# A four-layer gated decoder: tile weights of the first mixture of experts loaded inside the attention before it, and the router's steps rearranged

## What is computed

```python
def _L0_xattn_ref(Q_decoder, K_encoder, V_encoder, Wq, bq, ...):   # 16 heads of 8
    ...
    attn = jax.nn.softmax(scores, axis=-1)
    ...
def _L0_ffn_ref(x, router_w, w1, w2):        # 8 experts, 128 -> 512 -> 128
    probs = jax.nn.softmax(xf @ router_w.T, axis=-1)
    topv, topi = jax.lax.top_k(probs, 2)
    topv = topv / (topv.sum(axis=-1, keepdims=True) + 1e-09)
    cw = (jax.nn.one_hot(topi, e, dtype=xf.dtype) * topv[..., None]).sum(axis=1)
    h = jax.nn.gelu(jnp.einsum('td,edh->teh', xf, w1), approximate=False)
    y = jnp.einsum('teh,ehd->ted', h, w2)
    out = jnp.einsum('te,ted->td', cw, y)
x = x + jnp.tanh(g_xattn[0]) * _L0_xattn_ref(_layernorm(x, axis=-1), ctx_1024, ctx_1024, ...)
x = x + jnp.tanh(g_ffn[0]) * _L0_ffn_ref(_layernorm(x, axis=-1), ...)
```

## Time and profile before

| | us |
|---|---|
| median of 3 runs | 1693.77 (1693.45 to 1694.56) |
| the profiled execution | 1691.46 |
| its span from first to last instruction | 1689.7 |
| busy: PE / DVE / POOL / ACT | 1406.0 / 1081.6 / 780.9 / 681.7 |
| mean granted clock of TensorE | 0.925 of full |

### The profile page before, as it was taken

How to read it: one execution, slowest core, us unless ns; L and a number is a source line. 1 busy time by engine, 2 the same in 40 slices (tenths; PEclk the granted TensorE clock), 3 DMA queues, 4 the chain that set the end, 5 groups by cost and what they waited for, 6 DMA issues and landing times. The chain is left out here.

```text
span 1689.7 us, 34140 instructions
## 1 busy us (share of the span) xinstructions
PE 1406.0 (83%) x10919; PEld 1116.2 (66%) x10919; DVE 1081.6 (64%) x2418; ACT 681.7 (40%) x1663; POOL 780.9 (46%) x1037
## 2 busy tenths in 40 slices
PE   4999765989656785999978886899999999687996
PEld 3777655989655564666634444777878778587884
DVE  4888752414399687999958884455555855364455
ACT  3676442323343333556633332344455454421121
POOL 2554581345384353555533331444444577307355
PEclk9999897999855897999979999899999999889899
DMA  6400015758110000000000000000000000186952
GB/s 183 179 2 2 11 34 158 220 170 265 54 33 10 1 1 1 0 0 0 0 1 0 0 0 1 1 0 0 0 1 1 6 20 15 54 235 188 275 163 83
DMA packets 96487, 100.03 MB, mean 59 GB/s; under 512 B 12150, under 2 KB 69678, under 8 KB 95727
## 3 DMA queue, kind: packets, MB, share of 16 engines
q1 hardware_dynamic: 62322, 69.60, 13.6%
q0 software_dynamic: 8192, 16.79, 3.4%
q10 hardware_dynamic: 25852, 12.09, 2.5%
HBM read 72.23 MB, written 26.21 MB: 58 GB/s over the span
## 5 line engine op out<-in xcount | busy, mean ns | idle before, releaser
L439 POOL TENSOR_TENSOR exp_scores<-exp_scores,softmax_recip 128x308 f32<-128x308 f32 x256 | 181.7, 742 | 179.8 <-DVE softmax_recip L611 179.6
L633 PE MATMUL psum<-identity,exp_scores 128*77 128x128 f32 x1024 | 164.7, 287 | 37.6 <-POOL exp_scores L439 25.4
L1942 POOL TENSOR_TENSOR exp_scores_xattn<-exp_scores_xattn,softmax_recip_xattn 128x1640 f32<-128x1640 f32 x32 | 93.5, 2921 | 162.6 <-DVE softmax_recip_xattn L2115 162.6
L1201 PE MATMUL psum<-sorted_transposed_ffn,tile_weights_up_ffn 128*128 128x128 f32 x1280 | 164.7, 283 | 4.3 <-DVE sorted_transposed_ffn L1089 4.1
L633 PEld LDWEIGHTS psum<-identity,exp_scores 128*77 128x77 f32 x1024 | 123.2, 153 | 60.5 <-issue 28.9
L1201 PEld LDWEIGHTS psum<-sorted_transposed_ffn,tile_weights_up_ffn 128*128 128x128 f32 x1280 | 154.1, 197 | 11.6 <-DVE sorted_transposed_ffn L1089 11.4
L975 POOL DMA_INDIRECT gathered_rows_ffn<-sorted_y,slot_ffn x96 | 90.7, 944 | 105.4 <-DMA sorted_y<-expert_rows_ffn 46.4
L454 ACT COPY probs_transposed<-psum 77x512 f32<-77x512 f32 x192 | 111.2, 581 | 57.3 <-PE psum L633 55.4
L1211 PE MATMUL psum<-expert_weights_down_ffn,hidden_ffn 128*128 x960 | 123.7, 280 | 3.3 <-issue 2.9
L964 POOL DMA_INDIRECT sorted_x<-xn_ffn,slot_ffn x64 | 61.3, 957 | 139.3 <-DVE slot_ffn L851 120.4
L1211 PEld LDWEIGHTS psum<-expert_weights_down_ffn,hidden_ffn 128*128 128x128 f32 x960 | 115.8, 195 | 5.2 <-issue 5.2
(11 more groups left out here) (367 smaller groups left out, 3388.7 us busy)
## 6 DMA issues: line engine op xcount, KB each, us to landing
tile_weights_up_ffn<-in_L_ffn_packed_dram SPq DMA_DIRECT2D x160, 256.0 KB, 3.3
sorted_rows_ffn<-sorted_x SPq DMA_DIRECT2D x80, 128.0 KB, 3.7
sorted_y<-expert_rows_ffn ACTq DMA_DIRECT2D x80, 128.0 KB
sorted_x<-zeros SPq DMA_DIRECT2D x4, 1280.0 KB, 13.0
x_residual<-in_x_dram SPq DMA_DIRECT2D x4, 512.0 KB, 11.3
expert_weights_down_ffn<-in_L_ffn_packed_dram SPq DMA_DIRECT2D x8, 256.0 KB, 15.2
sorted_x<-xn_ffn,slot_ffn POOLq DMA_INDIRECT x128, 2.2
gathered_rows_ffn<-sorted_y,slot_ffn POOLq DMA_INDIRECT x128, 2.9
```

The costliest lines, as they stand in the source:

```text
L439: nc.gpsimd.tensor_tensor(e[:, par, heads, :], e[:, par, heads, :], rec.to_broadcast([S, HG, KC]), ALU.mult).then_inc(s["probs_ready"], 1)
L633: last = nc.tensor.transpose(m.psum[0:KC, 4 + g % 2, h * S:(h + 1) * S], e[:, nxt, g * HG + h, :], m.ident[:, :])
L1201: mm = nc.tensor.matmul(m.psum[:, 2 * (n % 2) + half, to:to + SUB], w[:, n % DEPTH, u, at:at + 128], xst[:, n % 2, u * SUB:(u + 1) * SUB], ...
L1942: nc.gpsimd.tensor_tensor(ev, ev, recip[:, par, :].unsqueeze(2).to_broadcast([S, H3, KV]), ALU.mult).then_inc(s["probs_ready"], 1)
```

## The change

It has three parts, all in layer 0.

1. SP waits within the attention for the tiles' expert numbers (`route_known`), and loads the up-weights of tiles 0 to 5 there. Their buffer is allocated before the attention, and the tile semaphores with it. In the mixture SP begins with the rows of tiles 0 to 5.
2. `xn_ffn` of the first half is written by ACT, with scale and bias per partition, after its last copy of the step, and no longer by DVE.
3. `pick_second` moves from step 23 to step 22, behind the reciprocal; counting and ranking move from step 24 to step 23, and the slots with them, behind that step's reciprocal; weights go from step 26 to 24, tile experts from 27 to 25. POOL's scatter begins in step 24.

```diff
-    PICK, COUNT = EXP + 1, EXP + 3
+    PICK, COUNT = EXP + 1, EXP + 2
     SCATTER = COUNT + 1
@@ attention, SP
+                    sync.wait_ge(s["route_known"], 1)
+                    for n in range(DEPTH):
+                        for u in range(TILE // SUB):
+                            e = sync.value_load(r.expert[0:1, 0, n * 2 + u:n * 2 + u + 1], min_val=0, max_val=E0 - 1)
+                            sync.dma_start(r.w_up[:, n, u, :], r.packed[bass.ds(e, 1), :, 0:F0].rearrange("o p c -> p (o c)")).then_inc(m.tile_loaded[r.layer][n], 16)
@@ attention, ACT, end of the step
+                    if at in NORMALISE_STEPS:
+                        g = NORMALISE_STEPS.index(at)
+                        act.wait_ge(s["route_shift"], 1 if g < PGROUPS - 1 else 2)
+                        for n in range(g * GB, (g + 1) * GB):
+                            ins = nc.scalar.activation(r.xn[:, n, :], m.x[:, n, :], ACT.Identity, scale=m.rstd2[:, n:n + 1], bias=m.shift2[:, n:n + 1])
+                        ins.then_inc(s["route_xn"], 1)
@@ attention, DVE, ahead of the sum
-                    if at in NORMALISE_STEPS:
...
-                            ins = nc.vector.tensor_scalar(r.xn[:, n, :], m.x[:, n, :], m.rstd2[:, n:n + 1], m.shift2[:, n:n + 1], ALU.mult, ALU.add)
...
-                    if at == PICK + 1:
-                        pick_second(nc, m, r, 0, link, s["route_picked"])
...
                     if at == COUNT + 1:
-                        slots_of_pairs(nc, m, r, 0, link, s["route_ranked"])
+                        weigh_experts(nc, m, r, 0, link)
                     if at == COUNT + 2:
-                        weigh_experts(nc, m, r, 0, link)
-                    if at == COUNT + 3:
                         expert_of_tiles(nc, m, r, 0, link, s["route_known"])
@@ attention, DVE, behind the reciprocal
+                    if at == PICK:
+                        pick_second(nc, m, r, 0, link, s["route_picked"])
+                    if at == COUNT:
+                        slots_of_pairs(nc, m, r, 0, link, s["route_ranked"])
@@ mixture, SP
-                for n in range(3):
-                    load_weights(n)
-                for n in range(3):
+                early = DEPTH if layer == 0 else 3
+                if layer == 3:
+                    for n in range(early):
+                        load_weights(n)
+                for n in range(early):
                     load_rows(n)
...
-                for n in range(3, NTILES):
+                for n in range(early, NTILES):
```

More of the change, by code:

```diff
@@ L133, in allocate @@
     m.gathered = {n: [ctx.enter_context(nc.semaphore(f"gathered_{k}_ffn{n}")) for k in range(4)] for n in (0, 3)}
+    m.tile_loaded = {n: [ctx.enter_context(nc.semaphore(f"tile_loaded_{k}_ffn{n}")) for k in range(DEPTH)] for n in (0, 3)}
     m.zeros = sb("zeros", [128, SLOT_ROWS, D])
@@ L572, in step @@
                         rstd_of_x(nc, m, dve, s["route_sd"], s["route_rstd"], s["route_shift"], lo, hi, 0 if lo == 0 else 1, True)
-                    if at in NORMALISE_STEPS:
-                        g = NORMALISE_STEPS.index(at)
-                        for n in range(g * GB, (g + 1) * GB):
-                            ins = nc.vector.tensor_scalar(r.xn[:, n, :], m.x[:, n, :], m.rstd2[:, n:n + 1], m.shift2[:, n:n + 1], ALU.mult, ALU.add)
-                        ins.then_inc(s["route_xn"], 1)
                     if at == PICK:
@@ L740, in __init__ @@
         self.w = sb("expert_weights_down", [128, E0, F0 // 128 * D]) if layer == 0 else None
+        self.w_up = sb("tile_weights_up", [128, DEPTH, TILE // SUB, F0]) if layer == 0 else None
         self.xn = sb("xn", [S, B, D])
@@ L871, in sparse_experts @@
              "exp_wanted exp_ready picked counted counts_read ranked tiles_known scale_ready "
-             "tile_loaded_0 tile_loaded_1 tile_loaded_2 tile_loaded_3 tile_loaded_4 tile_loaded_5 sorted_t_in_psum sorted_t_ready hidden_in_psum silu_ready hidden_ready "
+             "sorted_t_in_psum sorted_t_ready hidden_in_psum silu_ready hidden_ready "
              "y_in_psum y_ready y_stored_0 y_stored_1 combined link "
@@ L876, in sparse_experts @@
     scattered, gathered = m.scattered[layer], m.gathered[layer]
-    tile_loaded = [s[f"tile_loaded_{k}"] for k in range(DEPTH)]
+    tile_loaded = m.tile_loaded[layer]
     y_stored = [s[f"y_stored_{k}"] for k in range(2)]
@@ L890, in sparse_experts @@
         xs = sb("sorted_rows", [128, DEPTH, TILE // 128, D])
-        w = sb("tile_weights_up", [128, DEPTH, TILE // SUB, down_at])
+        w = r.w_up if layer == 0 else sb("tile_weights_up", [128, DEPTH, TILE // SUB, down_at])
         w_down = r.w if layer == 0 else sb("expert_weights_down", [128, E0, chunks * D])
```

## The result

| | before | changed kernel |
|---|---|---|
| median of the runs, us | 1693.61 (1691.34 to 1694.56, 4 runs) | 1677.12 (1676.69 to 1678.08, 4 runs) |
| ratio, with its 95% interval | | 0.9908 (0.9892 to 0.9923) |
| the profiled execution, its span, us | 1691.46, 1689.7 | 1676.69, 1674.9 |
| mean granted clock of TensorE | 0.925 | 0.932 |

One execution of the second timing, at 3047.74 us, was in a slow state and is left out of its numbers. Two readings of the traces answer where it comes from: the seam, and what lies behind it.

The account below looks back on a forecast made before the run. The bound was one chain from layer 0's attention into its mixture: POOL's last product, scatters, meeting, weight loads, rows, PE. Terms -8.2 - 3.8 + 0 + 2.0 = -10.0 us took 1693.77 to 1683.8, range 1679.8 to 1688.6.

Parts of the forecast that it names:

- the seam: Between layer 0's attention and mixture: POOL's last product, scatters, meeting, weight loads, rows, PE; all terms together -10.0 us.
- Part 1: Mixture opening: with weights already loaded, PE starts 3.0 us after the opening instead of 11.2, -8.2 us.
- Part 2: End of layer 0's attention: 8 scatters instead of 11 behind POOL's last product, 1.26 us each, -3.8 us.
- Part 3: Normalise in layer 0's attention, steps 15 to 20: ACT takes what DVE returns, 0 us.
- Part 4: Layer 0's attention, steps 22 to 25: picks and slots wait beside POOL's products, and PE's clock slows, +2.0 us.
- half-clock step: Steps 23 and 24: PE idles longer and comes out at half speed, slowing addition of the maximum and transposes, +1.0 us.
- not held: Picks and slots in steps 22 to 24: POOL does not hold DVE, sum -12.8, 1681.0 us; chance 0.19.
- whole row: Step 22's picks wait for POOL's whole row of products, sum about -7.8, 1686.0 us; chance 0.20 together with ACT deciding.
- so a microsecond at the seam is a microsecond of the time: Everything behind layer 0's attention: nothing later is tied to anything before the mixture, so the seam's -10.0 us carries over whole.
- TensorE stays at the low level: Layer 0's attention from step 23: granted clock stays at 1.2 GHz to its end, +24 us, 1708 us; chance 0.04.

Follow-up runs that it names:

- again: The changed kernel timed and profiled once more, unaltered: 1678.92 us, ratio 0.9918 to the kernel before.
- third: The changed kernel a third time, unaltered, as control for the dummy products: 1679.82 us, ratio 0.9926 to the kernel before.
- after_pad: The changed kernel plus a 0.38 us DVE fill ahead of its first operation of layer 3's attention: 1677.98 us, ratio 0.9912 to the kernel before.
- e1: The kernel before with only the early weight loads of six tiles: 1684.21 us, ratio 0.9941; its unaltered repeat 1685.86 us, 0.9960.
- weights_pad2: The kernel before with early weights alone, plus a DVE fill of some 0.75 us ahead of layer 3's attention: 1683.40 us, ratio 0.9941.
- warm_pad: The changed kernel with unread dummy products on PE at layer 0's seam, plus a 0.38 us DVE fill ahead of layer 3's attention: 1676.14 us, ratio 0.9911.
- no_act: The changed kernel with the normalise put back on DVE: 1681.26 us, ratio 0.9923 to the kernel before.
- no_picks: The changed kernel with picks, counts and slots in their old steps: 1682.54 us, ratio 0.9930 to the kernel before.
- warm: The changed kernel with 34 unread products on PE after layer 0's attention and 10 at the mixture's start: 1680.95 us, ratio 0.9937 to the kernel before.
- e2_normalise: The kernel before with only the normalise moved to ACT: 1692.32 us, ratio 0.9991.

## Why the prediction was right and wrong

**Part 1**, -8.2: right. PE started 2.85 us behind the opening where 3.0 were forecast, and right behind its register loads. The five traces of kernels that load weights in the mixture have 10.6 to 11.2 us there, mean 10.8, so the term measured -8.0. SP issued the twelve loads from 200.96 on for 13.62 us (forecast were 12.6, from about 200).

**Part 2**, -3.8: right. From POOL's last product to the opening, 19.43 us became 15.67: -3.76. The 15.5 us that the working gives for eleven scatters run from the start of POOL's last product to the start of the last scatter; the term rests on the 1.26 us of one.

**Part 3**, 0: right at the seam. With it alone POOL's last product began at 242.44 (242.46 before), and the time is the same (0.9978 to 1.0005). Its four operations cost ACT 1.65 us a step. In that trace DVE's reciprocals of steps 15 to 17 and 19 come 0.9 to 1.4 us earlier than before, those of steps 18 and 20 within 0.15 us of before: ACT took back what DVE returned. The slack was 1.7 us and not 1.5, since the row at 138.81 does not read ACT's copy and the next one, at 139.03, does. What the working did not have is this part's effect in layer 3, below.

**Part 4**, +2.0: the direction right, the size twice too large. The picks ended 3.3 us behind the reciprocal's start (forecast 3.4): three of the four with two SBUF inputs took 0.67 to 0.75 us beside POOL's products, where the same operations took 0.29 before. The rule cited from the Trainium skill ("SBUF — State Buffer", "Who interferes with whom") agrees with this. But the slots took 1.6 us and not 3.0. Each operation waited at most for the one product then running: the first of the slots' two-input operations had begun before POOL's product did, and their second, like the fourth pick, began 0.2 us before a product's end and took 0.39 us (0.37 before). The 2.30 us of line 1475 that the working leaned on covered two POOL products in a row (514.64 to 516.68), so it was no price for a wait of one. Step 23 came at 12.46 (11.5), step 24 at 8.06 (9.1), step 25's products at 27.9 (28.1). The 1.0 us for a half-clock step was spent inside step 23: the granted clock was 0.73 over that step, and DVE idled 1.46 us for PE's transposes where 0.6 were reckoned. What the slots saved paid for it, and from step 25 on POOL is the bound. Counted from step 22's reciprocal, POOL's last product stood at 68.6 us in both traces of before and at 69.2, 69.2, 69.4 and 69.9 in the change, again, third and after_pad: +0.6 to +1.3. Single executions scatter here: e1, without this part, has 70.1, its repeat 68.7. The rivals "not held" and "whole row" are both out.

So the seam, forecast at -10.0, measured -11.0, -12.5 and -11.2 in three traces of the change and -10.5 in after_pad, whose seam is the same. The 1 us or so by which most of them exceed the forecast is part 4. The 1.5 us by which `again` is ahead of the first it has already at step 22's reciprocal (172.87 against 174.32).

**The step that failed** is the sentence "so a microsecond at the seam is a microsecond of the time". It put everything behind the seam at nothing. It looked for waits that stay where they are when the work moves and found none, rightly; but the changes of TensorE's granted clock do not move with the work microsecond for microsecond. Of the some 14 us, some 11 are the seam and some 3 came on top, by two effects. One belongs to the execution: from the mixture's start to layer 2's end the three traces of the change went by -2.4, -2.6 and +0.3 us, and e1 and its repeat by +0.3 and -2.5. In the eighteen traces without dummy products the way from PE's first instruction of the mixture to its first of layer 3's attention took 759.6 to 762.8 us, and yet, as shown above, the clock falls at the same place behind that opening in all of them, to 0.2 us. So a microsecond at the seam does not come through as one in a single execution; how the phases between bring this about was not followed. The other belongs to the kernel: from layer 2's end on, nine traces with 3.04 us for the first queries' products gained 0.4 to 2.0 us against before (weights_pad2, the tenth, lost 0.9), and ten traces with 4.7 to 5.0 us stood from 0 to +3.6. That the place of the products against the clock's changes decides this is shown by weights_pad2 and warm_pad, where a fill that computes nothing turned it, and by the order of all twenty traces. Part 3 is what puts the change on the good side: no_act, without it, has products of 4.85 us, no_picks, with it, 3.04. It does so by a hair: the products of the change, again and third begin 0.02 to 0.11 us later against the clock's fall than those of warm, and warm and e2_normalise, which have part 3 too, stand on the other side. So this share of the gain is partly luck. Why DVE opens layer 3's attention 0.37 us later when it has 16 instructions fewer in layer 0 was not tried and stays open. The traces have one lead: where DVE normalises (nine traces), a transfer of instructions on queue 14 starts 7.7 to 8.9 us ahead of that opening; where ACT does (eleven), none does in the 12 us ahead of it, and one starts 1.0 to 1.1 us behind it.

The rival "TensorE stays at the low level" had the right engine and the wrong place: the clock was low for 6.8 us of step 23 and then at 2.4 GHz to the attention's last step; it fell or came back a few us sooner or later in layer 3, and for the better.

## What to carry to other kernels

A term-by-term sum along one seam can be right to a microsecond and the total still be 0.2% off: in this kernel, where TensorE idles often, its clock turned small shifts into jumps in phases that nobody had touched. So time a change together with a copy of it that is shifted by a fill, and trust the part of a gain that survives the shift. A row far behind the edit, such as one group of products whose length goes from 4.9 to 3.0 us, tells such a jump at once, where the totals of a few runs hardly do.

## What the runs showed of the hardware that was not expected

- Work added made a kernel faster: a fill of 0.38 us on DVE took 4.8 us off warm's median (two chips, before within 0.13 us on both). In the traces the difference, 5.1 us, lies behind layer 2's end, where the granted clock is higher.
- Identical products took 3.04 or 4.7 to 5.0 us as they began up to 1.1 us later or earlier behind the granted clock's fall; at the border (warm and third) 0.03 us lay between the two.
- Products that nobody reads, put into an idle stretch of 12 us, held PE's clock at 2.4 GHz through it and shortened tile 0's up products from 3.51 to 2.05 us; the gain was real locally and not safe globally.
- A DVE operation of two SBUF inputs that began before POOL's product did (186.95 against 187.11) was not held: 0.27 us. One that began 0.2 us before a product's end got in ahead of the next product of the same row (187.58, 0.39 us).
